# Two attentions of a four-layer sandwich: the heads' stacks turned by plain fp32r matmuls instead of transposes

## The reference

```
attention 0:  q, k, v = heads of 8 (16 heads) of LN(x) @ Wq, Wk, Wv + biases; q, k scaled to length 1
              state = q; twice: state = softmax(state @ k.T) @ v; then @ Wo + bo, + residual
experts 0:    shared expert + top 2 of 8 experts (hidden size 512)
attention 1:  windowed attention (windows of 64 tokens) + global attention, one v for both,
              a learned bias by key position, (wout + out) @ w_out + b_out
experts 1:    shared expert + top 2 of 16 experts (hidden size 64)
```

## Time and profile before

| | |
|---|---|
| median of 3 runs | 1807.33 us (1806.85 to 1808.82) |
| profiled execution, own time | 1805.99 us |
| its span, first to last instruction | 1804.2 us |
| mean granted TensorE clock | 0.946 |
| PE busy | 1519.9 us, 84% of the span |
| VectorE, ScalarE, GpSimd busy | 1197.0, 1019.0, 784.9 us |
| matmuls that turn stacks, second attention | 512 queries, 256 keys: L1013, mean 297 and 290 ns |
| matmuls that turn stacks, first attention | 384 queries and states, 128 keys: L409, mean 290 and 305 ns |
| fp32r scores of the first attention, L385 | 1024 calls, 512 + 512 matmuls in the trace |

### The profile page before, as it was taken

How to read it: one execution, slowest core, us unless ns; L and a number is a source line. 1 busy time by engine, 2 the same in 40 slices (tenths; PEclk the granted TensorE clock), 3 DMA queues, 4 the chain that set the end, 5 groups by cost and what they waited for, 6 DMA issues and landing times. The chain is left out here.

```text
span 1804.2 us, 37712 instructions
## 1 busy us (share of the span) xinstructions
PE 1519.9 (84%) x12057; PEld 1150.1 (64%) x12057; DVE 1197.0 (66%) x3314; ACT 1019.0 (56%) x1870; POOL 784.9 (44%) x1008
## 2 busy tenths in 40 slices
PE   2599999989999587998169989888988999589997
PEld 1366767667666466987046656666656666378886
DVE  2367777767766456997556766676767766556676
ACT  1388787777776255776026555555555666434332
POOL 7755564674652344996653334333333221101111
PEclk9899999999999699999569999999999999889999
DMA  5000000010010110222111111111111111000000
GB/s 189 19 19 19 17 19 19 23 31 20 25 36 15 33 56 24 72 71 58 67 39 35 36 39 29 30 34 31 31 31 32 30 31 31 4 1 6 12 10 20
DMA packets 75098, 60.50 MB, mean 34 GB/s; under 512 B 17088, under 2 KB 71104, under 8 KB 74560
## 3 DMA queue, kind: packets, MB, share of 16 engines
q1 hardware_dynamic: 70848, 50.21, 9.7%
q0 software_dynamic: 4096, 8.40, 1.6%
HBM read 20.01 MB, written 13.37 MB: 19 GB/s over the span
## 5 line engine op out<-in xcount | busy, mean ns | idle before, releaser
L1261 DVE TENSOR_REDUCE a_qt<-a_ps_m 128x2 fp32r<-128x512 f32 (+1 forms) x384 | 264.8, 690 | 161.9 <-PE a_ps_m L1047 113.6
L524 ACT ACTIVATE a_p<-a_ps_s 128x1024 f32<-128x1024 f32 x256 | 264.0, 1032 | 33.9 <-PE a_ps_s L385 27.3
L633 DVE TENSOR_REDUCE a_qt<-a_ps_m 128x2 fp32r<-128x512 f32 x256 | 176.6, 690 | 87.8 <-PE a_ps_m L396 85.4
L791 POOL TENSOR_TENSOR a_rn<-a_ss,a_half 128x16 f32<-128x16 f32 x64 | 186.2, 2916 | 1.4
L1047 PE MATMUL a_ps_m<-a_kpad,a_qs 128*128 128x512 f32 x256 | 130.3, 509 | 55.1 <-DVE a_qt L1261 50.9
L1174 ACT ACTIVATE a_pg<-a_ps_s 128x1024 f32<-128x1024 f32 x128 | 131.7, 1030 | 17.0 <-PE a_ps_s L1022 12.1
L403 PE MATMUL a_ps_o<-a_p,a_v 128*32 128x256 f32 x2048 | 137.1, 385 | 3.0 <-ACT a_p L524 1.6
L396 PE MATMUL a_ps_m<-a_kpad,a_qs 128*128 128x512 f32 x256 | 116.9, 457 | 15.3 <-DVE a_qt L633 13.3
L1047 PEld LDWEIGHTS a_ps_m<-a_kpad,a_qs 128*128 128x128 f32 x256 | 50.0, 195 | 104.8 <-DVE a_qt L1261 85.0
L1013 PE MATMUL a_ps_a<-ident,a_qt 128*128 128x128 f32 x512 | 109.6, 297 | 5.4 <-ACT a_qsm L1168 3.8
L1492 POOL COPY a_v<-a_vt 128x64 f32<-128x64 f32 x64 | 15.3, 239 | 223.4 <-PE a_ps_o L1124 223.3
(11 more groups left out here) (362 smaller groups left out, 4334.4 us busy)
## 6 DMA issues: line engine op xcount, KB each, us to landing
a_kpad<-a_ks SPq DMA_DIRECT2D x768, 32.0 KB, 1.9
f_xin<-xs SPq DMA_DIRECT2D x39, 128.0 KB, 2.1
ys<-f_yout SPq DMA_DIRECT2D x39, 128.0 KB, 2.1
w<-in_w SPq DMA_DIRECT2D x2, 2304.0 KB, 11.2
out_x<-X SPq DMA_DIRECT2D x8, 256.0 KB, 2.3
xs<-f_zero SPq DMA_DIRECT2D x15, 128.0 KB
wgu<-in_wgu SPq DMA_DIRECT2D x1, 1152.0 KB, 5.2
xs<-Z,r_at POOLq DMA_INDIRECT x64
```

Of the source, the lines that this page charges most:

```text
L524: nc.scalar.activation(probs[:, u % 2, 2 * c:2 * c + 2, :, :].rearrange("p a b c -> p (a b c)"), ps_s[:, n % 2, :], ACT.Exp).then_inc(exp_ ...
L633: nc.vector.tensor_reduce(qt2[:, k % 2, 2 * part:2 * part + 2, SHIFT], ps_m[:, :, :], AX.X, ALU.max, negate=True).then_inc(max_done, 1)
L791: nc.gpsimd.tensor_tensor(rn[:, part * c:(part + 1) * c], ss[:, part * c:(part + 1) * c], half[:, 0:c], ALU.pow).then_inc(rn_ready, 1)
L1261: nc.vector.tensor_reduce(dst, src, AX.X, ALU.max, negate=True).then_inc(max_done, 1)
```

## The change

`stacked` no longer casts the stack to fp32. Every turning of a stack (T1, T2, K, Q in the first attention, all that go through `stack` in the second) is now a plain matmul with the stack as stationary operand and an identity as moving operand, both fp32r; transposes of other tiles stay as they are. The fp32r identity `ident_r` is one more SBUF tile that lives through both attentions; VectorE makes it by a copy at the start of the first attention's program, and PE waits for it (`set_up`, 4). The bias `bo1` of the second attention moves from the tiles that are loaded at the start to those loaded at the second attention's start: it becomes the first of five loads that SyncE issues and awaits there.

```diff
@@ -85,7 +85,7 @@
 
 def stacked(v):
 
-    return v.rearrange("p n s -> p (n s)").bitcast(F32)
+    return v.rearrange("p n s -> p (n s)")
 
 
 def hold(eng, sem, value, passed):
@@ -367,6 +367,7 @@
         @block.tensor
         def _(pe):
             pe.wait_ge(a["loaded"], 16 * a["loads"])
+            pe.wait_ge(set_up, 4)
 
             def wait_b(st, task):
                 wait(pe, b_done, st.at(lambda k: b_count(k, task) - 1))
@@ -403,6 +404,13 @@
                         last = nc.tensor.matmul(ps_o[SLOT * j:SLOT * (j + 1), :], v32[:, u % RING, t, j, :],
                                                 probs[:, u % 2, j, t, :], start=t == 0, stop=t == TPB - 1)
                 last.then_inc(full, 1)
+
+            def turn_stacks(parts):
+
+                for t in range(TPB):
+                    last = nc.tensor.matmul(ps_a[:, t * P:(t + 1) * P], parts(t), a["ident_r"][:, :], start=True,
+                                            stop=True)
+                last.then_inc(a_full, 1)
 
             def transposes(out, parts, done):
                 for t in range(TPB):
@@ -430,7 +438,7 @@
                 if unit(k - 2):
                     pe.wait_ge(qt2_ready, st.at(lambda k: k - 1))
                     wait_a(st, "T1")
-                    transposes(ps_a, lambda t: stacked(qt2[:, k % 2, t * G:(t + 1) * G, :]), a_full)
+                    turn_stacks(lambda t: stacked(qt2[:, k % 2, t * G:(t + 1) * G, :]))
                 if unit(k - 4):
                     pe.wait_ge(exp_done, st.at(lambda k: chunks(k - 1, 3)))
                     wait(pe, o1_copied, st.at(lambda k: clip(k - 1, UNITS)))
@@ -458,7 +466,7 @@
                 if unit(k - 3):
                     wait_a(st, "T2")
                     pe.wait_ge(max_done, st.at(lambda k: 4 * (k - 2)))
-                    transposes(ps_a, lambda t: stacked(qt2[:, (k - 3) % 2, t * G:(t + 1) * G, :]), a_full)
+                    turn_stacks(lambda t: stacked(qt2[:, (k - 3) % 2, t * G:(t + 1) * G, :]))
                 if unit(k - 1):
                     pe.wait_ge(exp_done, st.at(lambda k: chunks(k - 1, 1)))
                     pe.wait_ge(v_ready, st.at(lambda k: k))
@@ -470,7 +478,7 @@
                     nb, g = (k + NG) // NG, r
                     pe.wait_ge(stacks_ready, st.at(lambda k: 2 * ((k + NG) // NG + 1)))
                     wait_a(st, "K")
-                    transposes(ps_a, lambda t: stacked(kt[:, nb % 2, t * H + g * G:t * H + (g + 1) * G, :]), a_full)
+                    turn_stacks(lambda t: stacked(kt[:, nb % 2, t * H + g * G:t * H + (g + 1) * G, :]))
                 maxima(st, 1)
                 if r == 2 and batch(b + 3):
                     pe.wait_ge(z1_ready, st.at(lambda k: k // NG + 4))
@@ -504,7 +512,7 @@
                     nb, g = (k + NG) // NG, r
                     pe.wait_ge(stacks_ready, st.at(lambda k: 2 * ((k + NG) // NG + 1)))
                     wait_a(st, "Q")
-                    transposes(ps_a, lambda t: stacked(qt[:, nb % 2, t * H + g * G:t * H + (g + 1) * G, :]), a_full)
+                    turn_stacks(lambda t: stacked(qt[:, nb % 2, t * H + g * G:t * H + (g + 1) * G, :]))
                 if unit(k - 1):
                     wait_b(st, "O1")
                     pe.wait_ge(o1_copied, st.at(lambda k: k))
@@ -586,6 +594,7 @@
             nc.vector.memset(qt2[:].rearrange("p a b c -> p (a b c)").bitcast(F32), 0.0).then_inc(set_up, 1)
             dve.wait_ge(set_up, 3)
             dve.wait_ge(a["loaded"], 16 * a["loads"])
+            nc.vector.tensor_copy(a["ident_r"][:, :], ident[:, :]).then_inc(set_up, 1)
 
             def normalise(x, mv, rs, n, out):
 
@@ -1058,7 +1067,11 @@
                 t0 = (u % NG) * G
                 half, kind = (u // NG) % 2, GLOBAL if task[1] == "g" else WINDOWED
                 wait_a(st, task)
-                transposes(ps_a, lambda t: stacked(src[:, half, kind, t * H + t0:t * H + t0 + G, :]), a_full)
+                for t in range(TPB):
+                    last = nc.tensor.matmul(ps_a[:, t * P:(t + 1) * P],
+                                            stacked(src[:, half, kind, t * H + t0:t * H + t0 + G, :]),
+                                            a["ident_r"][:, :], start=True, stop=True)
+                last.then_inc(a_full, 1)
 
             def project(st, task):
                 n = ("v", "wq", "wk", "q", "k").index(task)
@@ -2355,17 +2368,18 @@
 
         X, Z = sb("X", [P, TILES * D]), sb("Z", [P, TILES * D])
         early = ["ident", "wqkv", "wo0", "bqkv", "bo0", "ln_w", "ln_b"]
-        small = ["gate", "rev", "w_in", "wo1", "b_in", "bo1", "pos"]
+        small = ["gate", "rev", "w_in", "wo1", "b_in", "pos"]
         t = {n: sb(n, [P, args[n].shape[1]]) for n in early + small}
         loaded, later, last_loaded = sem("loaded"), sem("later"), sem("last_loaded")
         x_loaded, passed = [sem("x_first"), sem("x_rest")], sem("passed")
+        ident_r = sb("ident_r", [P, P], F32R)
         rows, gates = sb("rows", [P, 2 * TILES], U32), sb("gates", [P, 2 * TILES])
         xs = nc.dram_tensor("xs", (EXPERTS * REGION + SPARE * SLOT_T, D), F32, kind="Internal").ap()
         ys = nc.dram_tensor("ys", (SLOTS * SLOT_T, D), F32, kind="Internal").ap()
         x_dram = args["x"].rearrange("(n p) d -> p n d", p=P)
         X3 = X[:, :].rearrange("p (n d) -> p n d", d=D)
         cut = X_FIRST * TPB
-        ffn0, ffn1 = ["w1", "w2", "moe"], ["wgu", "wd", "router", "pick"]
+        ffn0, last = ["w1", "w2", "moe"], ["bo1", "wgu", "wd", "router", "pick"]
 
         def load(sp):
             sp.dma_start(X3[:, 0:cut, :], x_dram[:, 0:cut, :]).then_inc(x_loaded[0], 16)
@@ -2376,9 +2390,9 @@
                 sp.dma_start(t[n][:, :], args[n]).then_inc(later, 16)
 
         def load_last(sp):
-            for n in ffn1:
+            for n in last:
                 sp.dma_start(t[n][:, :], args[n]).then_inc(last_loaded, 16)
-            sp.wait_ge(last_loaded, 16 * len(ffn1))
+            sp.wait_ge(last_loaded, 16 * len(last))
 
         scattered, routed = sem("scattered"), sem("routed")
         with ExitStack() as first_layer:
@@ -2400,7 +2414,7 @@
                 route[n] = rb(n, [P, most, EXPERTS])
             for n in ("m1", "m2", "row1", "row2"):
                 route[n] = rb(n, [P, TILES])
-            first_attention(nc, X, Z, t["ident"], dict(passed=passed, 
+            first_attention(nc, X, Z, t["ident"], dict(passed=passed, ident_r=ident_r,
                 wqkv=t["wqkv"], wo=t["wo0"], bqkv=t["bqkv"], bo=t["bo0"], ln_w=t["ln_w"], ln_b=t["ln_b"],
                 x_loaded=x_loaded, loaded=loaded, loads=len(early), load=load, later=later,
                 laters=len(small + ffn0), xs=xs, route=route, scattered=scattered))
@@ -2408,9 +2422,9 @@
             first_ffn(nc, X, Z, t["ident"], dict(passed=passed, w1=t["w1"], w2=t["w2"], gate=t["gate"], rev=t["rev"],
                                                      moe=t["moe"], xs=xs, ys=ys, rows=rows, gates=gates, route=route,
                                                      scattered=scattered, routed=routed))
-        for n in ffn1:
+        for n in last:
             t[n] = sb(n, [P, args[n].shape[1]])
-        second_attention(nc, X, Z, t["ident"], dict(passed=passed, w=t["w_in"], wo=t["wo1"], b=t["b_in"], bo=t["bo1"], pos=t["pos"],
+        second_attention(nc, X, Z, t["ident"], dict(passed=passed, ident_r=ident_r, w=t["w_in"], wo=t["wo1"], b=t["b_in"], bo=t["bo1"], pos=t["pos"],
                                                     load=load_last, ys=ys, rows=rows, gates=gates))
         second_ffn(nc, X, Z, t["ident"], dict(passed=passed, wgu=t["wgu"], wd=t["wd"], router=t["router"], rev=t["rev"],
                                               pick=t["pick"]), out)
```

## The result

The changed kernel took 1816.44 us (median of 5 runs, 1815.27 to 1819.24), the kernel before 1808.82 beside it. The ratio is 1.0049, 95% interval [1.0034, 1.0064]. So the change costs 7 to 9 us. The profiled execution took 1818.52 us, its span was 1816.7, which is 12.5 more than the span before (1804.2).

What follows compares the result with a forecast made beforehand. In the second attention PE was taken to bound from the second to the fifth maxima matmul, VectorE around them. 8.6 + 3.4 + 0.2 = 12.2 us, from the median 1807.33, gave 1819.5 us, range 1811 to 1830.

Steps and rivals of the forecast that it cites:

- main case: Both attentions: longer fp32r weight loads stick out at some pairs on the path, 12.2 us slower with the other edits; chance 0.66.
- two passes: Every turning: the plain product runs as two records, 0.22 us more a pair, 70 us in all, 1878 us; chance 0.02.
- all pairs on the path: Both attentions: every turning pair, or nearly, delays the kernel, 27.6 us more, 1835 us; chance 0.17.
- exposed pair: Two turnings whose weight load was not done ahead: 0.49 us in place of 0.44, counted as 0.06 more.
- covered pair: Two turnings whose weights were loaded in time: matmuls 0.006 us longer, counted as 0.015 more with the next instruction.
- Kg: Second attention, the turning pair directly ahead of the fifth maxima matmul: on the path, 0.06 us more a step.
- lower bounds: Least price of a pair on the path: 0.015 us more, if the plain load hides as the transposing one does.
- The sum of the second attention, 8.6: Second attention: pairs on the path add 0.135 us a step, times 64 steps, 8.6 us.
- The same clock: Both attentions: the granted clock, 0.99 in the first and 0.97 in the second, stays as it was.
- the third rival: Both attentions: plain matmuls keep the clock up where transposes let it fall, 5 us faster, 1802 us; chance 0.06.
- The first attention, 3.4: First attention: pairs on the path add 0.21 us a batch of four steps, times 16 batches, 3.4 us.
- The other edits, 0.2: VectorE's making of the fp32r identity costs 0.2 us at the start; PE's wait and the moved bias cost nothing.

Runs made afterwards that it cites:

- e1: Changed kernel with every turning a transpose again, leaving only the fp32r identity, PE's wait for it and the moved bias; 1811.05 us, 0.9995 of the kernel before.
- e2: Changed kernel with the second attention's turnings transposes again, so plain turnings in the first attention only; 1811.22 us, 0.9993 of the kernel before.
- e3: Changed kernel with the first attention's turnings transposes again, so plain turnings in the second attention only; 1815.04 us, 1.0030 of the kernel before.
- e8: Changed kernel with every turning of a stack in transposing mode on fp32r tiles with the fp32r identity; 1792.92 us, 0.9964 of the kernel before.
- e9: The changed kernel measured once more, with nothing else altered; 1814.18 us, 1.0037 of the kernel before.
- e10: Changed kernel with each plain turning of the second attention moving the identity twice, 256 columns; 1814.21 us, 1.0046 of the kernel before.
- e11: Repeat of e8, transposing mode on fp32r tiles, at another time; 1797.51 us, 0.9941 of the kernel before.
- e6: Changed kernel with extra 256-column matmuls in the second attention, two ahead of Mg's pair and three ahead of Kw's; 1.0110 of the kernel before.
- e7: The same extra matmuls as e6, but with all turnings as transposes; 1.0082 of the kernel before.

## Why the prediction was right in its outcome and wrong in its account

**Slower, within the range: right.** 1816.4 us against 1819.5, range 1811 to 1830. The forecast's main case said that exposed loads, on the path, would cost 12.2 us. The measured medians are 7.6 us apart. That this lies in the range is partly luck, as follows. Two rivals were rightly dropped: one record to each turning rules out two passes, and the last step of the second attention starts 12.3 us later (1563.8 for 1551.5), not 27.6, which all pairs on the path would give.

**The weight load: right as a row, wrong as a price. This is the step that failed.** The prediction took 0.10 us of exposure from L385's products for an fp32r load, found the load at 192 ns, and made an exposed pair 0.49 us. It is 0.44. What was missed is a second difference between the two forms: how soon the second matmul follows the first. A transpose on fp32 is followed 0.11 us later (0.38 minus 0.27), an fp32r matmul 0.05 to 0.06 (0.33 minus 0.27). The prediction had kept the 0.11 for both. So a covered pair gains 0.05 and an exposed one breaks even. Covered by the shorter load is not always covered by the longer one, though: pairs behind a maxima matmul go from 0.38 to 0.33 us, but those behind a projection, which had taken 0.38 too, now take 0.42. One of these in the first attention, before and after:

```profile
413.28 0.38 PE L409 MATMUL a_ps_a<-ident,a_qt 128*128 128x128 f32 x2
...
412.94 0.42 PE L411 MATMUL a_ps_a<-ident_r,a_qt 128*128 128x128 f32 x2
```

Elsewhere the loads' extra comes out one instruction later, and only where that instruction has a 128-column load of its own. PE's weight loads around Kg's pair, before:

```profile
1137.64 0.20 PEld L1013 LDWEIGHTS a_ps_a<-ident,a_kt 128*128 128x128 f32 x2
1137.81 0.19 PEld L1052 LDWEIGHTS a_ps_m<-a_kpad,a_qs 128*128 128x128 f32 x1
```

and after:

```profile
1142.02 0.30 PEld L1071 LDWEIGHTS a_ps_a<-ident_r,a_kt 128*128 128x128 f32 x2
1142.24 0.19 PEld L1061 LDWEIGHTS a_ps_m<-a_kpad,a_qs 128*128 128x128 f32 x1
```

The maxima matmul's load starts 0.17 us after the pair's before and 0.22 after. Over all pairs, from the start of the second turning to the end of what follows, the median went from 508 to 559 ns for maxima matmuls (at the full clock and right behind the pair), 392 to 445 for scores, 384 to 436 for projections, and stayed at 606 to 608 for products, whose weights have 32 columns. Per pair, and leaving those behind a projection aside, this makes: covered and narrow behind it, -0.05; covered and a full load behind it, 0; exposed and narrow, 0; exposed and a full load, +0.05. The prediction's lower bounds, 0.015 for an exposed and for a covered pair, had excluded a gain, though no row spoke against a gain.

**The sum of the second attention, 8.6: right size, another cause.** Of the prices just read, only Kg's is seen on the path: between the fourth and the fifth maxima reduction a step takes 0.03 us longer, and between the second, third and fourth less than 0.01. The forecast had 0.06 each for Qg and Kg and 0.015 for Mw. The median batch moved by 0.00 us, and by 0.07 step against step, where the forecast needed 4 x 0.135 = 0.54. The check that it named for itself, "steps of the second attention longer by 0.1 to 0.15 us", failed in every step kind (-0.04, +0.05, +0.03, -0.04). That the five further dips of the clock made 6.8 us, and the attention came out 8.6 us longer as forecast, is luck.

**The same clock: wrong, and the third rival had the wrong sign.** The prediction let the clock matter only if plain matmuls kept it up where transposes let it fall, and the Trainium skill's page "TensorE: Matmul & The Clock Gate", "Part 4: PE-mode transpose", stood behind that: the transposing mode isn't counted as activity in the same way. Here the runs go the other way. The kernel with transposes had 20.5 us at half clock in the second attention (with e1 20.5, with e2 23.9), the one with plain matmuls 41.0, 34.1 and, in e3, 30.7; and e8, all transposes but quicker, 27.3. The timed runs say the same: 12.6 to 26 us more at half clock for e3, e9 and the change, 17.3 for e8. What these kernels share is that their turnings hold PE for a shorter time, and e10, which gave that time back at the turning itself, lost the dips. That this is why the clock falls is an inference: e11 had only 3.7 us more, and e6, which gave PE more to do elsewhere, kept the difference to e7. The prediction should have asked what PE does around a dip before it took the clock as given.

**The first attention, 3.4: wrong.** Its batches got shorter, not longer. The medians went from 32.21 to 31.94 us, but set step against step it is 0.08 us a batch, 1.3 us in all. Some of its pairs are covered and have products with narrow weights behind them; others stand behind projections and got longer. Of this the timed runs show nothing (e2 0.9993 against e1 0.9995), and the attention's whole length in the profile did not fall either (510.2 in e2): its dips went from 6.8 to 20.5 us. They vary from run to run in this attention (6.8 to 20.5 us in kernels that are alike there), so what the change did to them is not shown.

**The other edits, 0.2: right** within what e1 can tell.

**What stays open.** e2 and e3 together give 0.23%, the whole change 0.37 and 0.49%; with intervals of 0.12 to 0.15 either way that may be chance or an effect of the two together. At 0.29, time at half clock accounts for some two thirds to four fifths of the loss (e3: 3.7 of 5.4 us, e9: 5.4 of 6.7) and Kg's 0.03 us a step for up to 1.8 us more. Why the clock falls more often is open, as is the price of one dip ahead of time (0.6 to 1.4 us in the profiles). An experiment that takes away the dips alone was not found: e10, which did so, paid elsewhere. Transposing with fp32r was not tried on the tiles that are plain fp32 (the values' and the projections' transposes), which would first have to be rounded.

## What to carry to other kernels

An instruction has a price in three places, and all three are to be read from rows before one is swapped for another: its own length when its load was done ahead, how soon the next of its kind follows, and what the instruction behind it waits for. One profile is a sample: e6's showed the clock of the kernel before, and its five timed runs did not. When a swap changes operand type and mode together, try them apart: here the type alone was a gain (-0.4 to -0.6%) and the mode's loss hid it. And where a stretch already falls to the half clock after a wait, freeing PE may be no gain: look at the clock next to each wait that grows, and at the mean clock of all timed runs.

## What the runs showed of the hardware

- The weight load of a 128x128 tile is recorded at 142 ns in the transposing mode, for fp32 and for fp32r (e8), and at 191 to 199 ns for a plain fp32r matmul.
- In a covered pair, a second 128-column turning follows the first after 0.11 us in fp32, and after 0.05 to 0.06 in fp32r, in either mode. Transposing mode on fp32r has both advantages: 0.29 us for a covered pair, where fp32 takes 0.38.
- With quicker turnings TensorE's profiles show more time at the half clock in the second attention (20.5 us to 27.3 to 41.0), in further dips of 3.4 us that made their steps 0.6 to 1.4 us longer. With each turning twice as wide (e10) it was 20.5 again, and e10's timed runs had no more of it than those of the kernel before.
- Among the timed runs of one kernel, a microsecond more at the half clock goes with 0.29 us more time (153 runs).
- Five more matmuls of 256 columns a step are not hidden in waits of 0.5 and 0.9 us a step: they cost 0.23 us a step (e7).
